# An attention-and-experts kernel on one core: the head shared out anew, expert registers loaded before the gathered rows, token tiles in order of time, and all closing sums on VectorE

## The chip, the cores and the metric

One core of a Trainium2 chip. The metric is device time in microseconds (us), the median of the runs. Engines are named as in the profile: PE is TensorE (PEld its weight loads), DVE is VectorE, ACT is ScalarE, POOL is GpSimd, SP is SyncE, which here only issues transfers.

## What is computed

Input x has 2 sequences of 2048 tokens with 128 channels, 4096 tokens in all.

```
xn  = layernorm(x)
xm  = xn * time_mix + shift(xn) * (1 - time_mix)
k, v, r = exp(min(xm Wk', 60)), xm Wv', xm Wr'
wkv, sum_k = decayed running sums over time of k*v and of k
s   = (sigmoid(r) * wkv / sum_k) Wo'
e   = argmax(xn Wg + bg)            (one of 8 experts for each token)
g   = silu(relu(xn W1[e] + b1[e]) W2[e] + b2[e])
out = x + s * g
```

All matrices are float32. W1[e] is 128x512 and W2[e] 512x128.

## The kernel before, in words

The 4096 tokens are 32 tiles of 128 (`NT`), four tiles to a block of 512 (`TPB`, 8 blocks `NB`, 4 to a sequence, `NBB`). A block's tokens are dealt to partitions four in a row: partition p of block c holds tokens 4p to 4p+3, so that a load or a store of a block is one run of 2 KB on each partition. The helper `every(a, j)` takes each fourth column of a block, and puts a tile's columns back in order of time where a tile meets a transposed block: in `transposes` (output in PSUM), in `logits_by_token` and in `project` (stationary operand in SBUF).

Head. SP loads x in 8 pieces, then the projection weights, biases, W1 and W2. DVE takes the statistics of each tile (L499), in two halves; after each half it works out `rstd` and `nbias` (L505 to L523) with one square root on ACT (`deviation`, L770). The tiles are then normalised by three engines: of each block POOL does tiles 0 and 1 (L452), ACT tile 2 (L786), DVE tile 3 (L533). POOL comes to it behind its series for the decay (L435 to L444). PE transposes the tiles (`transposes`, L939), ACT copies them out (L793), PE forms the gate logits (L948), ACT copies those (L805), PE turns them by token (L957), and DVE picks experts and makes ranks and one-hot tables (L573 to L640). PE inverts the order with 32 small matmuls (L1028), after the first `INV_AFTER` = 8 of 24 k/v/r projections (`kvr`, L989). From this come `gidx` (rows to gather), `etab` (the expert of each slot), `ttab` and `sidx`. The normalised rows go to DRAM as `xn_rows` (L351), behind the load of W2 on SP's queue.

Loop. There are 39 slots (`SLOTS`): rows sorted by expert, 128 to a slot, some tiles run twice. POOL gathers rows (L460), PE transposes them (L1038), multiplies by W1 of the slot's expert (`layer1`, L1047), ACT applies bias and relu (L857), PE multiplies by W2 (`layer2`, bias at L1059, L1064), ACT copies (L866), POOL scatters to `g_rows` (L467). The first 12 slots also carry one projection each. The slot's expert sits in a register; registers are loaded eight at a time (`Picks.fetch_for`, L95). The first load on PE stands behind `transpose_rows(0)`, and `layer2` and `relu` form the index `e*HC+c` for each of their four parts. Meanwhile DVE does the running sums (`attend`).

Tail. When all scatters have landed, SP loads `g_rows` in 8 blocks (L370), ACT applies silu (L917), DVE multiplies by the projected attention (L748) that PE makes with 64 matmul passes (`project`, L1079), and x is added: by DVE (L753) for blocks 0, 2, 4, 6, 7, by POOL (L483) for blocks 1, 3, 5 (`POOL_SUMS`). SP stores each block (L376).

Of the kernel before, what the change touches and what calls it, by code (L numbers as in the profile page):

```python
# [31 lines left out]
POOL_SUMS = (1, 3, 5)  # L32
# [13 lines left out]
XLOADS = NB  # L46
# [4 lines left out]
INV_AFTER = 2 * NBB  # L51
# [4 lines left out]
TAYLOR = 9  # L56
SMALL_DECAY = 0.5
# [3 lines left out]
BK = 3 * BQ  # L61

# [40 lines left out]
def mixture_kernel(nc, x, time_decay, time_first, time_mix, Wk, Wv, Wr, Wo, Wg, bg, W1, b1, W2, b2, out):  # L103
    ctx = ExitStack()
    with ctx:
# [24 lines left out]
        w2 = sb("w2", [P, E * HC, P])  # L130
        wnat = sb("wnat", [P, 4, P])
# [11 lines left out]
        b1T = sb("b1T", [P, BQ])  # L143
        tmix = sb("tmix", [P, 1])
# [164 lines left out]
        out_pool = sem("out_pool")  # L309
# [20 lines left out]
        def _(sp):  # L330
            for j in range(XLOADS):
                sp.dma_start(x_sb[:, j * TPB:(j + 1) * TPB, :], x_v[:, j, :, :]).then_inc(ld_x[j], 16)
# [12 lines left out]
            sp.dma_start(w2[:, :, :], W2.rearrange("e (c p) d -> p (e c) d", p=P)).then_inc(ld_w2, 16)  # L345

            for b in range(BATCH):
                sp.wait_ge(xn_pool, NBB * (b + 1))
                sp.wait_ge(xn_dve, NBB * (b + 1))
                sp.wait_ge(xn_act, NBB * (b + 1))  # L350
                sp.dma_start(xn_v[:, b * NBB:(b + 1) * NBB, :, :],  # L351
                             xn_sb[:, b * HALF:(b + 1) * HALF, :].rearrange("p (c j) d -> p c j d", j=TPB)
                             ).then_inc(xn_stored, 16)
# [14 lines left out]
            for c in range(NB):  # L368
                tiles = slice(c * TPB, (c + 1) * TPB)
                sp.dma_start(g_sb[:, tiles, :], g_v[:, c, :, :]).then_inc(g_loaded[c], 16)  # L370
            for c in range(NB):
                if c in POOL_SUMS:
                    sp.wait_ge(out_pool, POOL_SUMS.index(c) + 1)
                else:
                    sp.wait_ge(out_dve, len([m for m in range(c + 1) if m not in POOL_SUMS]))
                sp.dma_start(out_v[:, c, :, :],  # L376
# [381 lines left out]
        def _(act):  # L758
# [51 lines left out]
            for k in range(NBB):  # L810
                normalise(k)
# [326 lines left out]
```

## Time and profile before

| what | value |
|---|---|
| median of 3 runs | 176.46 us (175.15 to 176.85) |
| the profiled execution, time | 175.93 us |
| its span, first to last instruction | 174.1 us, mean granted PE clock 0.963 |
| busy: PE, DVE, ACT, POOL | 149.5, 122.8, 102.4, 98.5 us |
| DMA moved | 27.96 MB, mean 161 GB/s |

The 1.8 us between span and time lie outside the instructions. Busy shares are averages over three stages with different limits: the head to about 45 us, the loop to about 153 us, and the tail.

### The profile page before, as it was taken

The page shows a single profiled execution, that of the slowest core. Times are in us where ns is not written, and L with a number is a line of the kernel's source. Part 1 is how long each engine was busy: PE and PEld are TensorE (multiplying, and loading weights), DVE is VectorE, ACT ScalarE, POOL GpSimd, SP SyncE. Part 2 cuts the span into 40 slices and gives each one's busy share as a digit, 9 for nine tenths or more (in the row PEclk, how much of TensorE's full clock was granted, in tenths as well). Part 3 has the DMA queues.
Part 4 walks back from the last instruction along what each step waited for, and adds up shares of the span by engine and source line. Part 5 has one row for each costly group of instructions (what it writes and reads, how often), then busy time and mean ns, then how long its engine had stood idle before and what let it go on. Part 6 is the DMA issues. An engine that isn't in the chain of part 4 may idle for free.

```text
span 174.1 us, 3350 instructions
## 1 busy us (share of the span) xinstructions
PE 149.5 (86%) x954; PEld 119.0 (68%) x954; DVE 122.8 (71%) x262; ACT 102.4 (59%) x295; POOL 98.5 (57%) x149
## 2 busy tenths in 40 slices
PE   7995899996797689995999794985999999999960
PEld 2433465442575477874789693885999999999960
DVE  2498994999999999999999999999600000000971
ACT  2946975976484366564782922744886677642720
POOL 7879920017777475764455876746564464460550
PEclk9999999999699969999699999999999999999997
DMA  4943999706354142342323631543645552115973
GB/s 80 318 155 136 386 295 341 292 3 210 106 166 124 34 161 90 109 168 85 111 86 116 211 105 49 171 147 105 230 153 178 175 178 96 45 45 184 361 297 120
DMA packets 15808, 27.96 MB, mean 161 GB/s; under 512 B 2952, under 2 KB 3520, under 8 KB 15792
## 3 DMA queue, kind: packets, MB, share of 16 engines
q1 hardware_dynamic: 12944, 23.10, 37.7%
q0 software_dynamic: 2272, 4.66, 9.5%
q8 instruction: 8, 0.13, 0.3%
q10 hardware_dynamic: 576, 0.01, 0.2%
q14 instruction: 8, 0.07, 0.1%
HBM read 10.78 MB, written 6.75 MB: 101 GB/s over the span
## 4 chain that ended last, share of the span: by engine, by line
PE 66%; issue 7%; ACT 6%; DMA 5%; POOL 4%; DVE 4%; another core or an unknown queue 3%; ACTq 2%; DVEq 0%
PE ps L1064 21%; PE ps L1047 20%; PE ps L1079 9%; PE ps L989 7%; DMA wg<-in_L_ffn_Wg 3%; PE ps L948 3%; DMA xg<-xn_rows,gidx 2%; PE ps L1038 2%; PE ps L939 2%; PE ps L1059 1%; ACT ohhi_hidif L857 1%; POOL ser L441 1%; DVE ohlo L607 1%; ACT kT L875 1%
## 5 line engine op out<-in xcount | busy, mean ns | idle before, releaser
L467 POOL DMA_INDIRECT g_rows<-gout,sidx x39 | 40.1, 1028 | 25.4 <-ACT gout L866 18.6
L460 POOL DMA_INDIRECT xg<-xn_rows,gidx x32 | 34.0, 1064 | 33.3 <-DVE gidx L658 15.8
L1047 PE MATMUL ps<-xn_sb,w1e 128*128 x312 | 43.7, 282 | 3.8 <-issue 3.7
L1047 PEld LDWEIGHTS ps<-xn_sb,w1e 128*128 128x128 f32 x312 | 39.9, 198 | 4.6 <-issue 4.6
L857 ACT ACTIVATE ohhi_hidif<-ps,b1T 128x128 f32<-128x128 f32 x104 | 30.2, 384 | 19.1 <-PE ps L1047 16.9
L1064 PE MATMUL ps<-w,ohhi_hidif 128*128 x208 | 29.6, 282 | 2.5 <-issue 2.5
L748 DVE TENSOR_TENSOR kT<-ps,kT 128x512 f32<-128x512 f32 x8 | 5.3, 688 | 37.3 <-ACT kT L917 36.4
L989 PE MATMUL ps<-xmT,wT 128*128 128x512 f32 x48 | 25.7, 649 | 4.5 <-ACT rT L877 1.9
L1064 PEld LDWEIGHTS ps<-w,ohhi_hidif 128*128 128x128 f32 x208 | 25.6, 192 | 5.6 <-issue 5.3
L866 ACT COPY gout<-ps 128x128 f32<-128x128 f32 x39 | 11.1, 284 | 15.7 <-remote 10.1
L857 ACT ACTIVATE hidT<-ps,b1T 128x128 f32<-128x128 f32 x52 | 15.0, 380 | 8.3 <-remote 4.2
L1064 PE MATMUL ps<-w,hidT 128*128 x104 | 16.2, 305 | 0.1
L1064 PEld LDWEIGHTS ps<-w,hidT 128*128 128x128 f32 x104 | 14.4, 214 | 1.9 <-issue 1.8
L1079 PE MATMUL ps<-wT,xnT 128*128 128x128 f32 x64 | 15.1, 397 | 0.0
L1079 PEld LDWEIGHTS ps<-wT,xnT 128*128 128x128 f32 x64 | 15.0, 330 | 0.0
L989 PEld LDWEIGHTS ps<-xmT,wT 128*128 128x128 f32 x48 | 8.3, 198 | 9.5 <-issue 5.6
L717 DVE RECIPROCAL ohlo<-ohlo 128x256 f32<-128x256 f32 x8 | 14.0, 1747 | 0.0
L721 DVE RECIPROCAL ohlo<-ohlo 128x256 f32<-128x256 f32 x8 | 13.9, 1741 | 0.0
L927 PE MATMUL ps<-ones 128*128 128x512 bf16 x46 | 11.8, 421 | 1.0 <-POOL ones L386 1.0
L499 DVE BATCH_NORM_STATS2 stats<-x_sb 128x6 f32<-128x128 f32 x32 | 7.3, 280 | 5.3 <-DMA x_sb<-in_L_attn_x 5.3
L698 DVE TENSOR_TENSOR_SCAN zk<-ps,zk,kT 128x512 f32<-128x512 f32 x8 | 10.2, 1276 | 0.0
L927 PEld LDWEIGHTS ps<-ones 128*128 128x128 bf16 x46 | 4.8, 106 | 7.5 <-issue 2.2
(165 smaller groups left out, 220.1 us busy)
## 6 DMA issues: line engine op xcount, KB each, us to landing
w1e<-w SPq DMA_DIRECT2D x39, 256.0 KB
x_sb<-in_L_attn_x SPq DMA_DIRECT2D x8, 256.0 KB, 6.1
w<-in_L_ffn_W SPq DMA_DIRECT2D x1, 2048.0 KB, 9.5
xn_rows<-xn_sb SPq DMA_DIRECT2D x2, 1024.0 KB, 12.4
kT<-g_rows SPq DMA_DIRECT2D x8, 256.0 KB, 4.4
out_x<-kT SPq DMA_DIRECT2D x8, 256.0 KB, 2.1
g_rows<-gout,sidx POOLq DMA_INDIRECT x39
xg<-xn_rows,gidx POOLq DMA_INDIRECT x32
```

Source lines behind the costliest of these rows:

```text
L460: g.indirect_dma_start(xg[j][:, :], None, xn_rows, bass.IndirectOffsetOnAxis(gidx[:, s:s + 1], 0)).then_inc(gathered[j], 16)
L467: g.indirect_dma_start(g_rows, bass.IndirectOffsetOnAxis(sidx[:, s:s + 1], 0), gout[j][:, :], None).then_inc(scattered[j], 16)
L698: v.tensor_tensor_scan(zk[:, 1:BLK + 1], decay(BLK), kT[:, here], zk[:, 0:1], ALU.mult, ALU.add).then_inc(dve_step, 1)
L717: v.reciprocal(rden[:, 0:BLK // 2], den[:, 0:BLK // 2]).then_inc(dve_step, 1)
L721: v.reciprocal(rden[:, half_b], den[:, half_b]).then_inc(dve_step, 1)
L857: last = s.activation(hidT[n % DEEP][:, cols], psH[n % DEEP][:, cols], ACT.Relu, bias=b1T[:, bass.ds(experts.of(n) * HC + c, 1)])
L866: s.copy(gout[n % OUT_RING][:, :], Y_BANK[n][:, 0:P]).then_inc(g_ready, 1)
L927: t.matmul(psS[:, :], ones[:, :], ones[:, 0:1].to_broadcast([P, BLK]), start=True, stop=True)
L989: last = t.matmul(bank_of(m)[:, :], wT[:, w, :], xmT[:, c * BLK:(c + 1) * BLK], start=True, stop=True)
L1047: last = t.matmul(psH[n % DEEP][:, cols], w1e[n % W1_RING][:, cols], xgT[:, bass.ds(held.of(n), 1), :].rearrange("p o t -> p (o t)"), star ...
L1064: last = t.matmul(Y_BANK[n][:, 0:P], hidT[n % DEEP][:, cols], w2[:, bass.ds(e * HC + c, 1), :].rearrange("p o d -> p (o d)"), start=False, ...
L1079: last = t.matmul(S_BANK[q][:, j * P:(j + 1) * P], every(rw[q], j), wT[:, 3, :], start=True, stop=True)
```

## The change

- Tokens: tile n is now 128 consecutive tokens, one to a partition. `every` goes; the transposes and the projection read and write 128 neighbouring columns. Loads of x and g, and the stores of xn and of the output, touch DRAM in runs of 512 B, four for what was one of 2 KB.
- Head: POOL normalises before its decay series, and also takes over the splitting of the b2 bias (8 small operations) from DVE. Tiles to engines: `POOL_TILES`, `DVE_TILES`, `ACT_TILES`, in all 12, 10 and 10 instead of 16, 8 and 8. ACT does `deviation(1)` ahead of its first copy, and mixes later. PE transposes the projection weights first. The inversion stands behind 10 projections instead of 8. The store of `xn_rows` goes ahead of the load of W2.
- Registers: on PE the loads for the first slots stand ahead of `transpose_rows(0)`, and `layer2` and `relu` index by the expert alone with a fixed part for c. The wait for W2 moves to slot 2.
- Tail: all eight closing sums on DVE.

```
-POOL_SUMS = (1, 3, 5)
-INV_AFTER = 2 * NBB
+TANH_AFTER = 2 * NBB
+INV_AFTER = TANH_AFTER + 2
+POOL_TILES = [(0, 1)] * NBB + [(0,)] * NBB
+DVE_TILES = [(3,)] * 2 + [()] * 2 + [(1, 3)] * NBB
+ACT_TILES = [(2,)] * 2 + [(2, 3)] * 2 + [(2,)] * NBB
...
-        x_v = x.rearrange("b (c p j) d -> p (b c) j d", p=P, j=TPB)
-        out_v = out.rearrange("b (c p j) d -> p (b c) j d", p=P, j=TPB)
-        xn_v = xn_rows.rearrange("(c p j) d -> p c j d", p=P, j=TPB)
-        g_v = g_rows[0:TOK, :].rearrange("(c p j) d -> p c j d", p=P, j=TPB)
-        every = lambda a, j: a.rearrange("p (q j) -> p j q", j=TPB)[:, j, :]
+        x_v = x.rearrange("b (n p) d -> p (b n) d", p=P)
+        out_v = out.rearrange("b (n p) d -> p (b n) d", p=P)
+        xn_v = xn_rows.rearrange("(n p) d -> p n d", p=P)
+        g_v = g_rows[0:TOK, :].rearrange("(n p) d -> p n d", p=P)
...
             for c in range(NB):
-                if c in POOL_SUMS:
-                    sp.wait_ge(out_pool, POOL_SUMS.index(c) + 1)
-                else:
-                    sp.wait_ge(out_dve, len([m for m in range(c + 1) if m not in POOL_SUMS]))
+                sp.wait_ge(out_dve, c + 1)
...
             deviation(0)
             for k in range(NBB):
                 normalise(k)
-            copy_xnT(0)
             deviation(1)
+            copy_xnT(0)
+            act.wait_ge(wT_ps, 1)
+            s.copy(wT[:, :, :].rearrange("p t d -> p (t d)"), psW[:, :]).then_inc(wT_ready, 1)
             copy_xnT(1)
+            normalise(4)
+            normalise(5)
+            copy_xnT(2)
+            normalise(6)
+            normalise(7)
+            copy_xnT(3)
             act.wait_ge(ld_small, 16 * 2)
             mix_here(0)
...
                 for c in range(HC):
                     cols = slice(c * P, (c + 1) * P)
                     last = t.matmul(Y_BANK[n][:, 0:P], hidT[n % DEEP][:, cols],
-                                    w2[:, bass.ds(e * HC + c, 1), :].rearrange("p o d -> p (o d)"),
+                                    w2_e[:, bass.ds(e, 1), cols].rearrange("p o d -> p (o d)"),
                                     start=False, stop=c == HC - 1)
...
-                    last = t.matmul(S_BANK[q][:, j * P:(j + 1) * P], every(rw[q], j), wT[:, 3, :],
+                    last = t.matmul(S_BANK[q][:, j * P:(j + 1) * P], rw[q][:, j * P:(j + 1) * P], wT[:, 3, :],
                                     start=True, stop=True)
...
             for m in range(INV_AFTER, EARLY):
                 kvr(m)
-            transpose_rows(0)
             pe.wait_ge(experts_ready, 1)
-            pe.wait_ge(bias_ready, 1)
-            pe.wait_ge(sel_ready, 3)
-            pe.wait_ge(ld_w2, 16)
             experts.fetch_for(0)
             pe.wait_ge(held_ready, 1)
             held.fetch_for(0)
+            transpose_rows(0)
+            pe.wait_ge(bias_ready, 1)
+            pe.wait_ge(sel_ready, 3)
```

## Rows read from the trace of the kernel before

**Rows 1.** The chain that ended last: start us, us, what.

```profile
13.72 1.80 POOL xn_sb L452 x4
...
21.72 0.75 PE ps L957 x4
22.47 0.44 PE ps L939 x4
...
40.19 3.18 DMA xg<-xn_rows,gidx
43.37 1.29 issue
...
153.45 14.95 PE ps L1079 x64
```

**Rows 2.** Groups by line and shape: busy us, mean ns, idle before.

```profile
L1047 PEld LDWEIGHTS ps<-xn_sb,w1e 128*128 128x128 f32 x312 | 39.9, 198 | 4.6 <-issue 4.6
...
L1079 PEld LDWEIGHTS ps<-wT,xnT 128*128 128x128 f32 x64 | 15.0, 330 | 0.0
```

**Rows 3.** VectorE in order of time in the tail: start us, us, operation.

```profile
160.76 1.32 DVE L748 TENSOR_TENSOR kT<-ps,kT 128x512 f32<-128x512 f32 x2 [35.94 <-ACT kT L917]
...
168.42 0.69 DVE L748 TENSOR_TENSOR kT<-ps,kT 128x512 f32<-128x512 f32 x1 [0.97 <-PE ps L1079]
169.03 1.28 DVE L753 TENSOR_TENSOR kT<-kT,x_sb 128x512 f32<-128x512 f32 x2
```

**Rows 4.** ScalarE in order of time in the tail.

```profile
160.00 1.28 ACT L917 ACTIVATE kT<-kT 128x512 f32<-128x512 f32 x2 [4.73 <-DMA kT<-g_rows]
162.37 3.90 ACT L917 ACTIVATE kT<-kT 128x512 f32<-128x512 f32 x6 [1.09 <-DMA kT<-g_rows]
```

**Rows 5.** DMA issues: count, KB each, median us to landing.

```profile
out_x<-kT SPq DMA_DIRECT2D x8, 256.0 KB, 2.1
```

**Rows 6.** Stretches: PE, PEld, DVE, ACT, POOL busy, granted clock, DMA share, GB/s.

```profile
22.00:30.00 8.00, 7.66 (x36) 4.55 (x36) 5.47 (x16) 5.11 (x10) 0.86 (x2) 1.00 1.05 313
30.00:33.00 3.00, 3.00 (x16) 1.47 (x15) 2.69 (x6) 2.91 (x6) 0.00 (x0) 1.00 1.05 409
```

**Rows 7.** VectorE in order of time, head, first half of x.

```profile
7.07 0.87 DVE L499 BATCH_NORM_STATS2 stats<-x_sb 128x6 f32<-128x128 f32 x4 [0.33 <-DMA x_sb<-in_L_attn_x]
...
8.42 0.15 DVE L553 TENSOR_SCALAR omt<-tmix 128x1 f32<-128x1 f32 x1 [0.48 <-DMA wg<-in_L_ffn_Wg]
```

**Rows 8.** ScalarE in order of time, head.

```profile
12.31 1.65 ACT L786 ACTIVATE xn_sb<-x_sb,nbias,rstd 128x128 f32<-128x128 f32 x4 [1.72 <-DVE nbias L523]
15.36 0.59 ACT L793 COPY xnT<-ps 128x512 f32<-128x512 f32 x1 [1.40 <-PE ps L939]
15.84 0.31 ACT L770 ACTIVATE std<-var,eps 128x16 f32<-128x16 f32 x1
```

**Rows 9.** PE in order of time, around the inversion.

```profile
31.99 4.54 PE L989 MATMUL ps<-xmT,wT 128*128 128x512 f32 x10
36.45 0.97 PE L1028 MATMUL ps<-ohhi_hidif,ohlo 128*128 128x32 f16 x24
37.66 0.36 PE L1028 MATMUL ps<-ohhi_hidif,ohlo 128*128 128x32 f16 x8 [0.24 <-DVE ohlo L607]
```

**Rows 10.** Register loads (L95): ns min/median/max, first and last start us.

```profile
L95 PEldq TENSOR_LOAD <-etab x5: 596/849/1546, 41.8 to 130.3; - x5
...
L95 PEldq TENSOR_LOAD <-ttab x5: 587/590/1125, 43.4 to 131.2; - x5
```

**Rows 11.** Stretches of the loop; columns as in group 6.

```profile
45.00:121.00 76.00, 64.20 (x428) 53.47 (x429) 75.70 (x128) 40.83 (x137) 49.54 (x47) 0.93 0.36 119
121.00:153.00 32.00, 32.00 (x288) 31.79 (x288) 3.82 (x6) 23.70 (x91) 17.38 (x18) 1.00 0.41 143
```

**Rows 12.** One line's instructions (L1064), its register operations.

```profile
L1064 PEldq FUSED_REGOPS  x156: 55/55/60, 51.6 to 152.2; - x156
```

**Rows 13.** A stretch at the start of the loop; columns as in group 6.

```profile
45.00:50.00 5.00, 5.00 (x22) 3.62 (x23) 4.96 (x13) 2.92 (x9) 4.09 (x4) 0.66 0.34 105
```

More of the change, by code:

```diff
@@ L45 @@
 SPARE = NS * P
-XLOADS = NB
+XLOADS = 8
 STAT = 6
@@ L61, with tiles_upto @@
 BK = 3 * BQ
+def tiles_upto(tiles, k):
+    return sum(len(tiles[m]) for m in range(k + 1))
 class Steps:
@@ L432, in _ @@
             g.tensor_copy(wgpad[:, :, 0:E], wg[:, :].unsqueeze(1).to_broadcast([P, TPB, E])).then_inc(wg_ready, 1)
+            for k in range(NB):
+                if k % NBB == 0:
+                    pool.wait_ge(ln_ready, k // NBB + 1)
+                for j in POOL_TILES[k]:
+                    n = k * TPB + j
+                    g.tensor_scalar(xn_sb[:, n, :], x_sb[:, n, :], rstd[:, n:n + 1], nbias[:, n:n + 1],
+                                    ALU.mult, ALU.add).then_inc(xn_pool, 1)
             pool.wait_ge(dec_ready, 1)
@@ L526, in finish_stats @@
                 dve.wait_ge(ln_ready, h + 1)
-            own_tiles = [n for n in range(NT) if n % TPB == 3]
+            own_tiles = [k * TPB + j for k in range(NB) for j in DVE_TILES[k]]
+            in_first = tiles_upto(DVE_TILES, NBB - 1)
             def normalise_tile():
@@ L557, in _ @@
             finish_stats(0, go_on=stats_tile)
-            for _ in range(len(own_tiles) // 4):
+            for _ in range(in_first):
                 normalise_tile()
@@ L749, in _ @@
                                     ALU.mult).then_inc(prod_ready, 1)
-                if c and c - 1 not in POOL_SUMS:
+                if c:
                     cols = slice((c - 1) * TPB, c * TPB)
@@ L811, in _ @@
                 normalise(k)
+            deviation(1)
             copy_xnT(0)
[L813 removed]
+            act.wait_ge(wT_ps, 1)
+            s.copy(wT[:, :, :].rearrange("p t d -> p (t d)"), psW[:, :]).then_inc(wT_ready, 1)
             copy_xnT(1)
+            normalise(4)
[4 more added lines that the diff above has]
+            copy_xnT(3)
             act.wait_ge(ld_small, 16 * 2)
             mix_here(0)
[L817 to L821 removed]
             act.wait_ge(ld_bg, 16 * TPB)
@@ L877, in copy_kvr @@
                     s.activation(rT[:, here], ps[:, :], ACT.Tanh, scale=0.5).then_inc(kvr_out, 1)
-            for m in range(INV_AFTER):
+            for m in range(TANH_AFTER):
                 copy_kvr(m)
@@ L883, in _ @@
             s.activation(sqrt_eps[:, :], eps[:, :], ACT.Exp)
-            for m in range(INV_AFTER, EARLY):
+            for m in range(TANH_AFTER, EARLY):
                 if m == EARLY - 1:
@@ L938, in transposes @@
                 for j in range(TPB):
-                    last = t.transpose(every(psT[k % 2][:, :], j), xn_sb[:, k * TPB + j, :], ident[:, :])
+                    last = t.transpose(psT[k % 2][:, j * P:(j + 1) * P], xn_sb[:, k * TPB + j, :], ident[:, :])
                 last.then_inc(xnT_ps, 1)
@@ L956, in logits_by_token @@
                 for i in range(TPB):
-                    last = t.transpose(psB[h][:, i * P:(i + 1) * P], every(lgT[:, h, :], i), ident[:, :])
+                    last = t.transpose(psB[h][:, i * P:(i + 1) * P], lgT[:, h, i * P:(i + 1) * P], ident[:, :])
                 last.then_inc(gates, 1)
@@ L990, in kvr @@
                 last.then_inc(kvr_ps, 1)
+            pe.wait_ge(ld_proj, 16 * 4)
+            for m in range(4):
+                last = t.transpose(psW[:, m * P:(m + 1) * P], wnat[:, m, :], ident[:, :])
+            last.then_inc(wT_ps, 1)
             transposes(0)
@@ L1008, in _ @@
             logits(7)
-            pe.wait_ge(ld_proj, 16 * 4)
-            for m in range(4):
-                last = t.transpose(psW[:, m * P:(m + 1) * P], wnat[:, m, :], ident[:, :])
-            last.then_inc(wT_ps, 1)
             logits_by_token(1)
```

95 lines of the change are left out of this document (37 added, 58 removed).

## The prediction

> **What bounds the kernel now.** I read the chain that ended last first, then each stage by the view that shows its limit. The chain is one path through three stages. In the head it runs over POOL's normalising, which starts at 13.72 although ACT had its numbers at 12.31, on through PE's transposes and logits, over DVE's tables and the inversion on PE, to the gathered rows: the second gather takes 3.18 us to 43.37, and the first matmul of the loop waits another 1.29 us for nothing that a semaphore shows [rows 1, 8]. The reader should see that the 1.29 us is PE's sequencer at two register loads, 1546 and 1125 ns at their slowest, the first of them at 41.8 [rows 10]. The loop has two parts: to 121 us PE works 64.20 of 76 us, from 121 to 153 all of 32 us [rows 11]. The tail begins at 153.45 with 14.95 us of `project` [rows 1]. The averages mislead here: PE looks like the bound of the tail, but two other things run through it. The loads of g let the first silu start at 160.00 [rows 4], and the DVE operations behind it follow each other at 0.60 to 0.63 us (1.32 less 0.69 for a pair of products, 1.28 less 0.68 for a pair of sums), from 160.76 until 170.31 [rows 3]. PE holds DVE up only before the last product, by 0.97 us.
>
> **The tail, part by part.** (1) `project`'s weight load took 330 ns on average with every fourth column, against 198 with neighbouring columns in L1047 [rows 2]; the passes came at 14.95/64 = 0.234 us, against 32/288 = 0.111 us in the packed part of the loop, where the weights lie in neighbouring columns [rows 11]; I take 0.12. So `project` shrinks to 64 x 0.12 = 7.6 us and ends near 161.1 instead of 168.4. By itself that is no gain of 7 us: what is late next is DVE. (2) DVE now has 16 operations instead of 13. I lay them out: product 0 at 160.76, product 1 at 161.39, sum 0 at 161.99; product 2 can't start before its silu ends, 162.37 plus (3.90/6) = 163.02 [rows 4], so it starts at 163.10; behind it stand 6 sums (1 to 6) and 5 products (3 to 7), then sum 7: 13 operations with product 2. Twelve steps of 0.60 put the last sum at 170.3 and its end at 171.0. Before, DVE ended at 170.31. So the tail loses 0.7 us by its own sum, although PE is freed by 7: three sums at 0.6 = 1.8 us eat the 0.97 us of waiting and more. Cover that is gone: POOL's adds were wholly hidden. (3) The loads and stores now touch DRAM in 512 B runs. W2's load already has such runs: around it (22 to 30 us, queues full) the DMAs moved 313 GB/s, right behind it with the 2 KB runs of `xn_rows` 409 GB/s [rows 6], a factor 1.31. On the last store, which lands in 2.1 us [rows 5], that is +0.3 us (bounds 0 and 1.31 x 2.1 = +0.65). The 4.2 MB of loads and stores need 4.2/0.313 = 13.4 us from about 158.5, that is to 171.9, ahead of the last store's landing near 173.5; so the queue isn't the bound, but close to it. Tail: +1.0 us, bounds +0.3 (sums packed a little denser, no cost of the runs) and +1.9 (silus late by the slower loads as well).
>
> The Trainium skill (DMA: Bandwidth & Descriptors, the table at its head) gives 512 B and above as enough for line rate, by which the runs of 512 B cost nothing. The two stretches above speak against it for this kernel. By it the tail would lose 0.7 us and the head's 0.6 us below would be nil.
>
> **The head.** (4) x arrives in 512 B runs. Third and fourth pieces matter: DVE waited for the third until 7.07, and then for the small constants until 8.42 [rows 7]. Between 5 us and there the transfers are what is waited for; 1.31 times as long puts the third piece at about 7.7 and the fourth at about 9.1, where its statistics now start at 8.5, right behind L553. +0.6 us (bounds 0, where the constants still come last, and +1.2). (5) POOL can now start at 12.3 instead of 13.72, so transposes stand ready 1.4 us earlier. But ACT now does `deviation(1)` ahead of the first copy, and that waits for the second half's statistics: it ran at 15.84, behind two fillers of DVE that are gone, so about 15.5; the first copy, at 15.36 before, comes at about 15.9 [rows 8]. With it, ACT's copy of wT and the four normalisings (0.39 us each, 1.65 for four) between the copies, the first logits come out 0 to 0.3 us later than before, not 1.4 earlier. The transposes that POOL frees have their cover in ACT's order. (6) The two `logits_by_token` took 0.75 us for four, with neighbouring columns they take 0.44 as L939 does [rows 1]: -0.6 us. Parts 5 and 6: -0.4 us, bounds -1.0 and +0.6.
>
> L939 also wrote PSUM with a stride, and still took 0.44 us for four [rows 1]. The Trainium skill (SBUF — State Buffer, the paragraph on cachelines) says that any access to PSUM that isn't contiguous slows matmuls markedly. By that rule the eight `transposes` would gain as `logits_by_token` does, some 0.3 us each where on the path; by the row I give them nothing.
>
> (7) The inversion now stands behind 10 projections. Before, it started at 36.45 exactly where the eighth ended and where its first table was ready, and its last part waited 0.24 us for DVE [rows 9]. Ten passes took 4.54 us with the last one drawn out, some 0.43 us from start to start, two to a projection, so two projections are 1.7 us: projections end 1.7 us later, the 32 small matmuls then run through in 1.3 us, and the result comes at about 39.5 instead of 38.0. +1.4 us (bounds +0.9, if PE starts this stretch earlier relative to DVE since wT is ready, and +1.7). Queued behind it are `gidx` on DVE, all of POOL's gathers, and SP's and ACT's register loads. (8) The register loads ahead of the rows: PE now loads while the gathers fly, the 1.29 us goes [rows 1]. What is late next is the second gather itself, so -1.3 us is the most, -0.6 the least. (9) Splitting b2 on POOL, the decay series later, `xn_rows` ahead of W2: all nil; POOL then idled from about 23 us to the gather at 38.6, W2 is first wanted in the loop, and DVE didn't lag there. If that cover went, the split would cost some 3 us before the gather. Head: 0.6 - 0.4 + 1.4 - 1.3 = +0.3 us.
>
> **The loop.** L1064 ran 156 register operations, 4 a slot, of 55 ns [rows 12]; `relu` forms its index 4 times a slot on ACT too. From 121 to 153 us PE is packed with them all in place [rows 11], so there they cost nothing. In the 11.8 us that PE stood idle before 121 some waits have no releaser in the trace; whether fewer register operations help there no row says. I take 0, bounds -4 (a third of the idle time) and +1.5 (such waits falling worse).
>
> **The sum** against the profiled execution: 175.93 + 1.0 (tail) + 0.3 (head) + 0 (loop) = 177.3 us. That execution is 0.5 us under the median of the runs and inside their spread, so 177.3 stands for the median too, 0.5% above it. No change can be told from one within 1% (174.7 to 178.2).
>
> **The rivals.**
> - *The loop's idle time shrinks.* Fewer instructions in PE's and ACT's streams, and a loop that begins without the 2.8 us gap that preceded a granted clock of 0.66 [rows 13]. For: waits without releaser fall inside L1064 and L1047. Against: the packed part. 3.5 us of the 11.8: 177.3 - 3.5 = 173.8.
> - *The runs of 512 B cost nothing* (the skill's rule): 177.3 - 0.6 - 0.3 = 176.4. Against it, rows 6; those stretches differ in more than the run, so it keeps a chance.
> - *It doesn't do what it says*: `project` stays bound by its weight loads. Then DVE waits for PE as now and only the last sums and the runs remain: tail +0.3, 176.6.
> - *Slower: PE's clock falls in the head.* Transposes 0 and 1 are now done by about 15.3 and PE waits for ACT's first copy until 16.5 or, with x late, 17.1; with the gap after the warm-up matmuls it works little from 12.8 to 17. PE's gap from 41.8 to 44.66 [rows 1, 10] preceded the stretch at 0.66 of full clock [rows 13], that is partly at 1.2 GHz. If it falls here, the four logits and two transposes on the path, 4 x 2 passes of 0.43 [rows 9] + 2 x 0.44 [rows 1] = 4.3 us, run at half speed for most of their length: +2 us, 179.3. It decides from the point where the first copy is later than about 17.
>
> **How the numbers follow.** Forecast 0.42 (its own range 175.6 to 178.9), shrinking loop 0.22, free runs 0.11, no faster weights 0.05, clock 0.20. The range 173.4 to 180.0 takes in all centres and the bounds of the tail and head, and leaves out the far end of the loop's. Faster by over 1%: the 0.22 and a little of the forecast, 0.25. Slower by over 1%: 0.20 and the upper quarter of the forecast, 0.32. Within 1%: 0.43.
>
> **What will show it.** L1079's passes at 0.12 us and PE done near 161 while the last DVE operation ends later than 170.31; 16 DVE operations from about 160.8 almost without a gap; the fourth piece of x waited for at about 9; GB/s near 310 where x, xn and g move; the first ACT copy at about 16.5 behind L770; the inversion's end 1.4 us behind the last table; no gap for register loads ahead of the loop. The forecast is wrong if the loop from its first L1047 to the first L1079 isn't 108.5 us within 1.5, if the granted clock leaves 1.0 in the head, or if the g loads rather than DVE order the tail.

## The result and the profile after

The changed kernel takes 182.03 us (median; 180.44 to 185.0) against 175.86 for the kernel before (175.15 to 176.85), a ratio of 1.039 with an interval of 1.031 to 1.048. The forecast was 177.3 with a range up to 180.0, so the loss is real and larger than anything the range allowed. The profiled execution took 182.01 us with a span of 179.9; 174.1 was the span before.

Split the span at two instructions, the first pass of the expert loop and the first pass of `project`, and the place of the loss is plain:

| | before | after | difference | forecast |
|---|---|---|---|---|
| head, to the first pass of L1047 / L1044 | 44.9 | 44.9 | 0.0 | +0.3 |
| loop, to the first pass of L1079 / L1076 | 108.4 | 113.6 | +5.2 | 0 |
| tail, to the end of the span | 20.8 | 21.4 | +0.6 | +1.0 |

The loop of the kernel before is counted here to 153.29, where the first pass starts by the records; the chain's 153.45 gives the 108.5 of the prediction.

The tail came out within 0.4 us of what was written. Groups by line and shape, after (columns as in [rows 2]):

```profile
L1076 PEld LDWEIGHTS ps<-wT,xnT 128*128 128x128 f32 x64 | 7.2, 192 | 0.0
```

The weight load fell from 330 to 192 ns, and the 64 passes end 7.3 us behind their start at 158.49. VectorE in order of time in the tail, after (answers to [rows 3]):

```profile
166.29 1.49 DVE L742 TENSOR_TENSOR kT<-ps,kT 128x512 f32<-128x512 f32 x2 [40.22 <-ACT kT L914]
167.70 0.68 DVE L747 TENSOR_TENSOR kT<-kT,x_sb 128x512 f32<-128x512 f32 x1
168.97 0.69 DVE L742 TENSOR_TENSOR kT<-ps,kT 128x512 f32<-128x512 f32 x1 [0.59 <-ACT kT L914]
...
175.57 1.28 DVE L747 TENSOR_TENSOR kT<-kT,x_sb 128x512 f32<-128x512 f32 x2
```

It never waits for PE; after its one wait of 0.59 us for ScalarE it is packed and ends at 176.85, 18.4 us behind the start of `project` against 17.0 before. ScalarE shows why it starts late (answers to [rows 4]):

```profile
165.53 0.63 ACT L914 ACTIVATE kT<-kT 128x512 f32<-128x512 f32 x1 [5.06 <-DMA kT<-g_rows]
166.35 0.63 ACT L914 ACTIVATE kT<-kT 128x512 f32<-128x512 f32 x1 [0.19 <-DMA kT<-g_rows]
168.24 0.63 ACT L914 ACTIVATE kT<-kT 128x512 f32<-128x512 f32 x1 [1.25 <-DMA kT<-g_rows]
```

Seven silus wait for a piece of g, two did before [rows 4]. The DMA issues of the page say the same, against 4.4 us for g before and 2.1 for the stores [rows 5]:

```profile
kT<-g_rows SPq DMA_DIRECT2D x8, 256.0 KB, 5.2
out_x<-kT SPq DMA_DIRECT2D x8, 256.0 KB, 2.6
```

The head, by the chain that ended last, after (start us, us, what):

```profile
37.91 0.81 PE ps L1025 x32
...
38.74 0.20 DVE gidx L652
38.94 0.03 POOLq L486
38.97 0.83 issue
39.80 1.37 POOL xg L475
...
41.47 3.04 DMA xg<-xn_rows,gidx
44.51 0.14 issue
```

The wait of 1.29 us for register loads [rows 1] is 0.14 here; the first gather starts at 39.80, where before it started at 38.6. Steps (7) and (8) can both be read off. Now the loop, by stretches (columns as in [rows 6]; answers to [rows 11] and [rows 13]), after:

```profile
45.00:50.00 5.00, 5.00 (x21) 3.86 (x21) 4.96 (x11) 3.16 (x10) 3.78 (x5) 0.55 0.37 120
52.00:66.00 14.00, 7.83 (x37) 5.83 (x37) 13.93 (x23) 4.88 (x15) 6.42 (x8) 0.78 0.27 89
45.00:121.00 76.00, 62.75 (x422) 53.23 (x422) 74.99 (x127) 40.54 (x135) 47.34 (x47) 0.90 0.35 114
```

and the same middle stretch of the kernel before:

```profile
52.00:66.00 14.00, 10.61 (x60) 8.45 (x59) 13.93 (x24) 6.03 (x20) 9.69 (x10) 0.88 0.33 105
```

Between 52 and 66 us PE makes 37 matmuls instead of 60. What happens there, ScalarE in order of time (its L854 is `relu`), after:

```profile
52.37 0.40 ACT L846 COPY xn_sb<-ps 128x256 f32<-128x256 f32 x1
59.03 1.14 ACT L854 ACTIVATE hidT<-ps,b1T 128x128 f32<-128x128 f32 x4 [6.26 <-remote]
```

and before:

```profile
53.69 1.14 ACT L857 ACTIVATE hidT<-ps,b1T 128x128 f32<-128x128 f32 x4 [1.43 <-remote]
55.20 0.59 ACT L875 COPY kT<-ps 128x512 f32<-128x512 f32 x1 [0.37 <-remote]
59.56 0.27 ACT L866 COPY gout<-ps 128x128 f32<-128x128 f32 x1 [3.77 <-remote]
```

and PE, after:

```profile
51.14 1.06 PE L1044 MATMUL ps<-xn_sb,w1e 128*128 x8
...
54.00 1.06 PE L1044 MATMUL ps<-xn_sb,w1e 128*128 x8
61.22 2.08 PE L986 MATMUL ps<-xmT,wT 128*128 128x512 f32 x2 [6.17 <-ACT kT L872]
```

and SyncE, which waits for the same semaphore before it issues the next copy of W1, after:

```profile
59.02 0.49 SPq L370 DMA_DIRECT2D w1e<-w  x1
```

"Remote" is the profile's word where it finds no releaser. The `relu` at 59.03 is that of the third slot (the `relu`s of the first two start at 47.08 and 50.36). It waits for `hid_ps`, and by the records the third slot's W1 passes ended at 52.20. Two engines that wait for this semaphore go on within 0.01 us of each other, 6.8 us later. So ScalarE isn't what is slow: the signal itself, PE's, comes late, or the passes ended later than the records say, for the ends of matmuls are modelled. PE's next projection then waits for ScalarE until 61.22. Before has such waits of ScalarE in three parts, 5.6 us together. PE stands idle for 6.2 of these 14 us after and for 3.4 before, and that difference alone is larger than the whole forecast.

A count of matmuls in a window depends on where it ends (from 45 to 121 us it is 422 against 428 [rows 11], for the kernel before stands still twice just ahead of 121), so here is the lag of the changed kernel slot by slot, at the first W1 pass: 0.0 us at the first slot, 3.7 at the seventh, 3.1 at the 24th, 5.2 at the 26th, and 5.2 at the last. So 3.7 of the 5.2 us are lost before the seventh slot, and the rest around the 25th, where PE stops three times between 121.8 and 124.4 us, for 2.05 us in all.

The register operations that I hoped would be fewer are not. One line's instructions, after:

```profile
L1061 PEldq FUSED_REGOPS  x156: 46/46/46, 52.2 to 157.3; - x156
```

Still 156, 46 ns each where they took 55 [rows 12].

### The profile page after: what moved, and what is told of

Read it like the earlier page. It is cut to its first block, busy times and chain, and to the rows that moved or that the text cites. A ratio compares the mean times of both kernels' runs of the same rounds, so it can differ in the third digit from the quotient of the medians.

```text
span 179.9 us, 3350 instructions
## 1 busy us (share of the span) xinstructions
PE 143.1 (80%) x954; PEld 113.6 (63%) x954; DVE 122.9 (68%) x259; ACT 102.9 (57%) x297; POOL 93.8 (52%) x150
## 3 DMA queue, kind: packets, MB, share of 16 engines
q1 hardware_dynamic: 25232, 23.10, 39.8%
## 4 chain that ended last, share of the span: by engine, by line
PE 59%; DMA 8%; ACT 8%; DVE 7%; issue 6%; another core or an unknown queue 5%; POOL 2%; ACTq 2%; SPq 1%; DVEq 0%; POOLq 0%
PE ps L1044 20%; PE ps L1061 19%; PE ps L986 10%; PE ps L945 4%; DMA wg<-in_L_ffn_Wg 3%; DMA kT<-g_rows 3%; ACT ohhi_hidif L854 2%; DVE stats L510 2%; PE ps L1035 2%; DVE kT L742 2%; DMA xg<-xn_rows,gidx 2%; DVE kT L747 1%; ACT hidT L854 1%; DMA g_rows<-gout,sidx 1%
## 5 line engine op out<-in xcount | busy, mean ns | idle before, releaser
L482 POOL DMA_INDIRECT g_rows<-gout,sidx x39 | 39.8, 1021 | 27.7 <-ACT gout L863 22.5
L475 POOL DMA_INDIRECT xg<-xn_rows,gidx x32 | 33.1, 1036 | 31.3 <-DVE gidx L652 10.9
L1044 PE MATMUL ps<-xn_sb,w1e 128*128 x312 | 45.0, 288 | 2.5 <-issue 2.5
L1044 PEld LDWEIGHTS ps<-xn_sb,w1e 128*128 128x128 f32 x312 | 41.3, 205 | 3.3 <-issue 3.1
L854 ACT ACTIVATE ohhi_hidif<-ps,b1T 128x128 f32<-128x128 f32 x104 | 29.9, 377 | 20.5 <-PE ps L1044 18.5
L742 DVE TENSOR_TENSOR kT<-ps,kT 128x512 f32<-128x512 f32 x8 | 5.5, 688 | 40.9 <-ACT kT L914 40.8
L1061 PE MATMUL ps<-w,ohhi_hidif 128*128 x208 | 30.7, 293 | 1.4 <-issue 1.4
L1061 PEld LDWEIGHTS ps<-w,ohhi_hidif 128*128 128x128 f32 x208 | 27.2, 203 | 4.6 <-issue 4.3
L854 ACT ACTIVATE hidT<-ps,b1T 128x128 f32<-128x128 f32 x52 | 15.1, 380 | 13.4 <-remote 6.3
L1061 PE MATMUL ps<-w,hidT 128*128 x104 | 15.4, 294 | 0.0
L1061 PEld LDWEIGHTS ps<-w,hidT 128*128 128x128 f32 x104 | 13.5, 203 | 1.3 <-issue 1.2
L1056 PE MATMUL ps<-b_rows,sel 96*128 96x128 bf16 x39 | 8.9, 229 | 3.1 <-ACT gout L863 3.1
L1035 PE MATMUL ps<-ident,xg 128*128 128x128 f32 x32 | 7.4, 312 | 3.7 <-DMA xg<-xn_rows,gidx 3.7
```

Of the source, the lines that this page charges most:

```text
L475: g.indirect_dma_start(xg[j][:, :], None, xn_rows, bass.IndirectOffsetOnAxis(gidx[:, s:s + 1], 0)).then_inc(gathered[j], 16)
L482: g.indirect_dma_start(g_rows, bass.IndirectOffsetOnAxis(sidx[:, s:s + 1], 0), gout[j][:, :], None).then_inc(scattered[j], 16)
L854: last = s.activation(hidT[n % DEEP][:, cols], psH[n % DEEP][:, cols], ACT.Relu, bias=b1T_e[:, bass.ds(experts.of(n), 1), c:c + 1].rearran ...
L1035: last = t.transpose(psX[:, (n - first) * P:(n - first + 1) * P], xg[n % RING][:, :], ident[:, :])
L1044: last = t.matmul(psH[n % DEEP][:, cols], w1e[n % W1_RING][:, cols], xgT[:, bass.ds(held.of(n), 1), :].rearrange("p o t -> p (o t)"), star ...
L1061: last = t.matmul(Y_BANK[n][:, 0:P], hidT[n % DEEP][:, cols], w2_e[:, bass.ds(e, 1), cols].rearrange("p o d -> p (o d)"), start=False, sto ...
```

## The experiments

Two things must be known to read them. The kernels of one set ran on one chip, and the chips are not alike: on two of the chips of these sets, as in the runs of the result, the kernel before takes 176 to 177 us; on the three others 157. So each ratio is against the kernel before on the same chip, and sets are not mixed. And a single profile stands for each run, while ratios rest on several executions.

### First set: the parts one by one (kernel before: 157.38 us)

e1, the kernel before with the new token layout and nothing else:

```
-x_v = x.rearrange("b (c p j) d -> p (b c) j d", p=P, j=TPB)
+x_v = x.rearrange("b (n p) d -> p (b n) d", p=P)
-last = t.matmul(S_BANK[q][:, j * P:(j + 1) * P], every(rw[q], j), wT[:, 3, :],
+last = t.matmul(S_BANK[q][:, j * P:(j + 1) * P], rw[q][:, j * P:(j + 1) * P], wT[:, 3, :],
```

> The kernel before with the new token layout alone (loads, stores, transposes, projection and the order of the tokens; head, registers and sums as before). Theory A (the 512 B runs of the layout pay for most of the loss, in the g loads, and the projection's gain finds no use): +1.5 to +3 us on 175.9, g loads landing at about 5.2 us each where it was 4.4, loop from the first L1047 to the first projection pass near 108.5 us. Theory B (the loss of 5 us sits in the loop and comes from how the loop is entered: register loads ahead of the rows, projections before the inversion): -1 to +1 us, loop 108.5 us. Theory C (the order of the tokens itself makes gathers and the loop slower): +5 us, loop near 113 us.

e2, the changed kernel with the old layout (the same lines the other way).

> The changed kernel with the old token layout (four tokens to a partition, 2 KB runs, strided projection), all else as changed. Theory A: about 178 to 179, the g loads at 4.4 us, but the tail again bound by 15 us of projection. Theory B: 181 to 182, loop near 113.5 us. Theory C: 177, loop near 108.5 us.

e3, the changed kernel with three of the closing sums on GpSimd again:

```
+POOL_SUMS = (1, 3, 5)
```

> The changed kernel with the closing sums of blocks 1, 3 and 5 back on POOL. If VectorE's order bounds the tail (my sum: three sums at 0.6 us): -1.5 us against the changed kernel. If the landings of the g loads bound it, which came 0.85 us apart in the changed kernel: -0.6 us or less. The loop is not touched under any theory.

e4, the changed kernel with the register loads behind the first transposes and the old index form again:

```
+transpose_rows(0)
+pe.wait_ge(bias_ready, 1)
+pe.wait_ge(sel_ready, 3)
+pe.wait_ge(ld_w2, 16)
 ...
-transpose_rows(0)
-b1T_e[:, bass.ds(experts.of(n), 1), c:c + 1]
+b1T[:, bass.ds(experts.of(n) * HC + c, 1)]
```

> The changed kernel with registers as before: loads behind the first transposed rows, index e*HC+c, wait for W2 before the loop. Theory A and C: +1 us (the loop begins 1.3 us later), loop length unchanged near 113.5 us. Theory B: the loop falls back to about 108.5 us, total 178 to 179.

| | time | ratio to before | interval | span | last VectorE operation to the end |
|---|---|---|---|---|---|
| e1 layout alone | 157.87 | 1.004 | 1.001 to 1.007 | 155.1 | 4.8 |
| e2 all but the layout | 157.86 | 1.001 | 0.997 to 1.005 | 155.6 | 2.5 |
| e3 all but VectorE's sums | 159.24 | 1.011 | 1.005 to 1.017 | 157.2 | 4.8 |
| e4 all but the registers | 159.18 | 1.011 | 1.005 to 1.017 | 157.1 | 3.1 |

The expectations named times near 176 us, so on this chip only their differences can be read, and the changed kernel itself isn't in this set. No part costs 4% here, and none of these traces has a hole like the one above. The gain of step (8) is seen in e4 against e2: with the register loads behind the rows the loop starts at 46.25 against 45.29 us, and `project` at 136.25 against 135.25.

The weight load fell to 192 ns with the layout alone (330 in e2), and it bought nothing. What it met in the tail are two other things, and four traces part them. From VectorE's last operation to the end it takes 4.8 us in e1 and e3 (512 B runs, GpSimd's sums kept), 3.1 in e4 (512 B runs, all sums on VectorE), 2.5 in e2 (2 KB runs, all sums on VectorE) and 3.8 in the trace of the kernel before, on a slower chip (2 KB runs, GpSimd's sums). So the shorter runs cost 0.6 to 1.0 us there and GpSimd's sums 1.3 to 1.7. In e1 GpSimd's last sum, of block 5, starts at 147.31 and takes 1.64 us, and the stores go out in the order of the blocks, so those of blocks 5, 6 and 7 leave together. Against that VectorE's end comes about 1 us later with all the sums (16.5 and 16.9 us behind the start of `project` in e1 and e3, 17.8 in e2 and e4). In sum, moving the sums to VectorE didn't lengthen the tail with 512 B runs, where the prediction has it do so: 21.4 and 21.8 us in e1 and e3 with GpSimd's sums, 20.9 in e4 without; on slower chips 22.4 in e7 and 22.4 in e6. The runs of 512 B by themselves, e4 against e2 on one chip: a piece of g lands after 4.8 us against 4.4, a store after 2.7 against 2.1, and the tail is 0.5 us longer.

### Second set: the changed kernel again, the inversion, the sums (kernel before: 177.21 us)

> The changed kernel itself, to be compared on the chip of this call with the kernel before. The first four experiments ran both parents at 157 to 159 us, where the pair of the result was at 176 and 182, and their traces have hardly any waits without a releaser in the loop. Theory L (most of the 5 us lost in the loop are such waits, which are a matter of the chip and fall otherwise in each kernel): here +1.0 to +1.5%, 158.9 to 159.8 us. Theory B (the way into the loop costs 5 us on any chip): +3% or more.

> The kernel before itself, for its trace on this chip: loop from the first L1047 to the first projection pass near 90 us under theory L, its head as in the trace shown (first L1047 at about 44.9 us), tail bound by the projection. Ratio 1.00.

e5, the changed kernel with the inversion where it was:

```
-INV_AFTER = TANH_AFTER + 2
+INV_AFTER = TANH_AFTER
```

> The changed kernel with the inversion behind 8 projections again. By my step 7 (the inversion waits for two projections) the first L1047 comes 0.7 to 1.4 us earlier than in the changed kernel and the time falls by as much. If the register loads or the gathers' own pace hold the loop's start: no change.

e6, the kernel before with the layout and all sums on VectorE (`POOL_SUMS` gone):

> The kernel before with the new token layout and all sums on VectorE. Against the layout alone (+0.4%): +0.5 to +1 us if VectorE's order bounds the tail, nil if the landings of the g loads do.

The changed kernel gave 181.62 us, 1.028 (1.018 to 1.037); the kernel before against itself 1.009 (1.002 to 1.015), which is how far such a comparison can be off on this chip (its profiled execution took 178.25 us, where the median of its ten is 176.9); e5 179.9, 1.018 (1.007 to 1.028); e6 177.14, 0.999 (0.994 to 1.005). So layout and sums together are free, and what is left for the loss is the head's order, the inversion and the registers. The kernel before itself has a loop of 111.3 us in this profile, where the first had 108.4. Ten projections ahead of the inversion cost what was forecast: in e5 the loop starts at 43.86, 45.20 in the changed kernel, 1.3 us. But putting it back didn't take the hole away.

### Third set: are the stalls VectorE's doing? (kernel before: 176.32 us)

In the traces so far of the slower chips PE's last gaps ended at 119 to 125.5 us, little before VectorE's running sums (`attend`) did, at 124 to 127, and PE was packed from there on. I took that for a cause.

x1, the changed kernel with these sums behind the loop:

```
+cap_keys(1)
+dve.wait_ge(hid_ps, SLOTS - 1)
```

> The changed kernel, but VectorE waits for the second-last slot of the expert loop before its running sums, so they no longer run beside the loop; output unchanged, the sums then stand between loop and projection. Theory A (TensorE and ScalarE stall in the loop only where VectorE works at its running sums beside them): the loop from the first L1047 to its last slot's matmuls falls from 112 to 114 us to 88 to 92, with hardly a gap over 0.55 us, and the time rises all the same, by about 40 to 60 us, since the sums come behind. Theory B (the stalls belong to the loop's own work: instruction fetch, transfers of gather and scatter, the clock): the loop keeps its 20 us of gaps. If before runs near 157 us in this call, no stalls are there to take away and the loop is about 90 us by both.

x2, the changed kernel, and x3, the kernel before, with the sums' numerators and decay in SBUF:

```
-decay_ps, num = psG[:, 0:1], psG[:, 1:BLK]
+decay_ps, num = sb("decay_sb", [P, 1])[:, :], ohlo_f[:, 2 * BLK:3 * BLK - 1]
```

> The changed kernel with the decay and numerators of VectorE's running sums in SBUF in place of the PSUM bank psG. Theory A1 (VectorE's reads and writes of PSUM hold up the matmuls): the loop loses most of its 20 us of gaps, 160 to 168 us where the changed kernel has 180 to 182. Theory A2 (the stalls go with VectorE's sums wherever they lie, in SBUF too, or with its instruction stream): 178 to 184, gaps near 21 us. Where before runs near 157: between 157 and 160 by both.

> The kernel before with the same move of decay and numerators from PSUM to SBUF. Theory A1: loop 90 to 95 us in place of 108, time 158 to 164. Theory A2: 175 to 179, ratio to before 0.99 to 1.01. Where before runs near 157: ratio 0.99 to 1.01 by both.

e7, the kernel before with the layout and the registers ahead:

> The kernel before with the new token layout and the register loads ahead of the rows; order of the head, place of the inversion, sharing of the normalising and POOL's sums as before. Theory C (the cost of the change comes with the later inversion and the reordered head, which shift VectorE's sums against TensorE's slots): first L1047 about 1.0 us earlier than before's, near 43.5, loop 106 to 109 us, time ratio 0.98 to 1.0. Theory D (the token layout with the registers' new place, another index form and code, disturbs the loop by itself): loop 111 to 114 us and ratio 1.01 to 1.03. Where before runs near 157: 0.99 to 1.0 by C.

x1 took 251.06 us (ratio 1.43). Its stretches, the third and fourth column pair being VectorE and ScalarE:

```profile
52.00:66.00 14.00, 7.04 (x35) 4.63 (x34) 0.00 (x0) 5.53 (x18) 6.68 (x7) 0.83 0.30 95
66.00:125.00 59.00, 52.36 (x373) 46.42 (x373) 1.23 (x1) 33.37 (x112) 35.29 (x36) 0.92 0.36 121
```

VectorE does next to nothing, and PE makes 35 matmuls from 52 to 66 as with it (37), 373 from 66 to 125 as with it. ScalarE's hole is there too:

```profile
61.83 1.14 ACT L854 ACTIVATE hidT<-ps,b1T 128x128 f32<-128x128 f32 x4 [4.71 <-remote]
```

The theory is dead: PE's gaps end at 125.2 us without VectorE's sums too. x2 (179.18, 1.020; 1.008 to 1.032) and x3 (177.42, 1.004; 0.993 to 1.015) fit that. e7 gave 177.63, 1.014 (1.002 to 1.026): its loop starts at 43.0, 1.2 us earlier than e1's and 1.0 earlier than e6's, which is step (8) as forecast, and its time gains nothing from it. Its loop of 110.2 us lies between what its two theories had (106 to 109 and 111 to 114), so it decides between them for neither.

All profiles of the slower chips side by side, matmuls in two stretches, and the time from the first slot's first W1 pass to the seventh's and from there to the last slot's. Two traces of the other chips stand below for comparison:

| | span | first gather | 52 to 66 us | 66 to 125 us | first to seventh slot | seventh to last |
|---|---|---|---|---|---|---|
| kernel before | 174.1 | 38.6 | 60 | 374 | 23.1 | 81.4 |
| kernel before again | 176.4 | 38.3 | 45 | 371 | 25.1 | 82.3 |
| x3 | 175.0 | 38.3 | 68 | 366 | 22.6 | 83.1 |
| e6 | 173.6 | 38.0 | 55 | 385 | 22.5 | 80.8 |
| e7 | 175.6 | 38.0 | 48 | 373 | 24.4 | 81.8 |
| changed kernel | 179.9 | 39.8 | 37 | 366 | 26.8 | 82.9 |
| changed kernel again | 179.5 | 40.0 | 28 | 373 | 28.5 | 79.8 |
| e5 | 176.7 | 38.7 | 28 | 380 | 27.9 | 79.8 |
| x2 | 178.7 | 40.9 | 50 | 363 | 25.9 | 80.7 |
| x1 (sums behind the loop) | 249.4 | 40.9 | 35 | 373 | 27.7 | 81.5 |
| e1, no stalls | 155.1 | 38.0 | 99 | 508 | 17.3 | 68.3 |
| changed kernel (z2 below), no stalls | 156.3 | 40.1 | 99 | 498 | 17.2 | 68.9 |

The two columns at the right tell it. To the seventh slot the five kernels with the old head need 22.5 to 25.1 us, the five with the new one 25.9 to 28.5, 3.8 us more on average and without overlap. From there to the last slot both kinds need the same, 81.9 and 80.9 us. (e7 has the registers ahead and stands with the old head, e5 has the inversion back and stands with the new one.) So most of the loss is a hole at the loop's start, not a slower loop. The 12 us by which the rest of the loop is slower here than on the other chips fall on both kernels alike. In the ten traces ScalarE's third `relu` starts at 53.0 to 55.8 us with the old head and at 55.0 to 61.8 with the new one; where it comes after 59, SyncE goes on within 0.05 us of it. In z2 it comes 0.5 us behind the records of its passes, at 52.35.

### Fourth and fifth set: are they GpSimd's gathers? (kernel before: 157.3 and 157.28 us)

In nine of the ten traces ScalarE's long waits at the loop's start end 0.2 to 2.4 us behind the first 14 gathers, which GpSimd issues one behind the other. In eight of the ten, PE's last gap over 0.55 us in the loop ended 2.7 to 4.5 us behind the start of the last gather (in x2 and in the kernel before again it came before it). So I changed the gathers.

y1, the changed kernel with plain copies, which bring each slot other rows than its own, so that the output is no longer that of the reference:

```
-g.indirect_dma_start(xg[j][:, :], None, xn_rows,
-                     bass.IndirectOffsetOnAxis(gidx[:, s:s + 1], 0))
+g.dma_start(xg[j][:, :], xn_rows[s * P:(s + 1) * P, :])
```

> The changed kernel, but GpSimd's 32 gathers by index are plain copies of rows 128s to 128s + 127 of xn_rows from the same queue, with the same waits and sizes, so each slot computes on other rows than it should. Theory G (TensorE and ScalarE are held up while GpSimd issues its gathers by index back to back, 14 of them from 40 to 58 us): ScalarE's hole of 6 to 8 us that ends at 59 to 62 us goes, slot 5 starts 9 to 10 us behind slot 3 in place of 15 to 17, and the loop shortens by 5 us or more. Theory H (the hole belongs to the loop's own first slots and projections): slot 5 starts 14 to 17 us behind slot 3 as before. Where before runs near 157 us there is no hole to take away.

y2 and y6, the changed kernel with `SCATTER_LAG = 3` and `9` in place of 5:

> The changed kernel with SCATTER_LAG 3 in place of 5: the first burst of gathers has 12 in place of 14 and the first scatter comes two gathers sooner. Theory G: the burst and the hole end some 2.5 us sooner, slot 5 starts 12 to 13 us behind slot 3, time 2 us less than the changed kernel's ratio of 1.03 to 1.04. Theory H: no difference, ratio to before 1.03 to 1.04.

> The changed kernel with SCATTER_LAG 9 in place of 5: up to 18 gathers before the first scatter. Theory G: the hole lasts longer, by what GpSimd's longer run of gathers allows (each pair behind the tenth waits for TensorE), slot 5 starts 16 to 20 us behind slot 3, time 1 to 4 us above the changed kernel's. Theory H: slot 5 as in the changed kernel, 14 to 17 us behind slot 3, time within 1% of it.

y3, the changed kernel with 4 buffers for gathered rows in place of 8:

> The changed kernel with 4 buffers for gathered rows in place of 8: the first burst has 4 gathers, then each pair waits for TensorE's transposes, 10 gathers before the first scatter. Theory G: the hole ends about 5 us sooner or breaks up, and the later stalls, which end 3.4 us behind the last gather in every run so far, end with the last gather again, which is now issued for slot 28 in place of 24, so that the last gap over 0.55 us comes later in the loop, at slots 27 to 29. Theory H: hole as in the changed kernel, last gap at slots 22 to 24 as before.

They fell on a chip without stalls, and so did the repeat of y1 with the changed kernel beside it:

> The changed kernel with GpSimd's gathers by index replaced by plain copies of rows from the same queue (each slot computes on other rows than it should), once more, since the first time it ran on a chip where before takes 157 us and no stall is there to take away. If before runs near 177 us here: theory G (the gathers hold up TensorE and ScalarE) gives slot 5 at 9 to 10 us behind slot 3 and a loop of 90 to 105 us; theory H (the hole belongs to the loop's own first slots) gives 14 to 17 us and a loop of 108 to 114. If before runs near 157 again, 156 to 160 by both, and what makes the stalls stays open.

> The changed kernel itself, beside the run with plain copies. Where before runs near 177 us: ratio 1.03 to 1.04, loop 111 to 114 us, slot 5 some 15 to 17 us behind slot 3. Where before runs near 157 us: the loop's share of the loss is gone and head and tail alone are left, ratio 1.005 to 1.015, loop 89 to 91 us.

| | time | ratio | interval |
|---|---|---|---|
| y1 plain copies | 158.08 | 1.005 (of the medians) | |
| y2 lag 3 | 161.61 | 1.028 | 1.020 to 1.036 |
| y3 four buffers | 167.34 | 1.056 | 1.045 to 1.066 |
| y6 lag 9 | 160.65 | 1.020 | 1.011 to 1.029 |
| z1 plain copies | 156.84 | 0.994 | 0.991 to 0.998 |
| z2 changed kernel | 159.26 | 1.016 | 1.012 to 1.020 |

The question about the stalls stays open with that. But z2 shows something else: without any stall the change still costs 1.6%, 2.0 us between the medians, a little more than the 1.005 to 1.015 expected of it. GpSimd's waits from 60 to 130 us (what waited for what: us in total, times, longest), z2:

```profile
POOL g_rows L482 <- issue: 9.1, 30, 0.3
POOL xg L475 <- issue: 4.9, 16, 0.3
POOL g_rows L482 <- ACT gout L863: 0.9, 3, 0.3
POOL xg L475 <- PE ps L1035: 0.6, 2, 0.3
```

51 pauses and none over 0.3 us: GpSimd waits for nobody, it issues its 71 gathers and scatters one behind the other, one in 1.38 us on average, from 40.1 to the last scatter at 136.9, and the loads of g wait for that scatter. In e1 it runs from 38.0 to 135.2. PE is as full as GpSimd, in the same trace (columns as in [rows 6]):

```profile
66.00:125.00 59.00, 58.99 (x498) 55.45 (x497) 58.81 (x95) 43.05 (x156) 46.51 (x42) 1.00 0.50 169
```

So neither has slack on such a chip. The first gather's start, by the chain of e1:

```profile
37.53 0.11 DVE gidx L656
37.64 0.32 issue
37.97 1.26 POOL xg L458
```

and by that of z2:

```profile
39.01 0.20 DVE gidx L652
39.24 0.83 issue
40.08 1.36 POOL xg L475
```

2.1 us later: 1.5 for gidx (the inversion for the most part), 0.5 for a longer pause of GpSimd ahead of its first gather, 0.83 instead of 0.32, in all traces with the new head whose chain shows it; its cause I didn't test. Of these 2.1 us 1.0 is left where the loop starts (the register loads give back 1.2), 1.5 where `project` starts, 1.7 at the first load of g, and 1.2 at the end of the span. It isn't the whole 1.6% either: e2 has its first gather as late (40.17) and is level with the kernel before.

z1 tells less than it seems. With plain copies GpSimd needs 0.55 us for an issue instead of 0.97 (medians) and waits for the others:

```profile
POOL g_rows L481 <- ACT gout L862: 18.1, 20, 1.2
POOL xg L475 <- PE ps L1034: 7.1, 7, 1.7
```

The changed kernel falls from 159.26 to 156.84, under the kernel before. But the first rows land sooner too: in the profiles the loop starts 1.3 us earlier (43.93 against 45.23), and is only 0.8 us shorter (89.2 against 90.0). By these two traces GpSimd's pace costs the loop about 0.8 us. y2 and y3 show from the other side how little slack there is. PE's waits in y3, 46 to 125 us:

```profile
PE ps L1036 <- DMA xg<-xn_rows,gidx: 4.1, 4, 1.7
```

With fewer gathers issued ahead PE runs into GpSimd's pace, and the loop takes 98.4 us instead of 90.0. With lag 9 (y6) the loop keeps 89.6 us, but the scatters come late, the last one at 138.3. Neither lag is faster than 5.

On the slower chips GpSimd has slack, for PE and ScalarE fall behind it. Its waits, same stretch, changed kernel:

```profile
POOL xg L475 <- PE ps L1035: 9.0, 5, 3.3
POOL g_rows L482 <- ACT gout L863: 7.5, 7, 2.8
POOL xg L475 <- remote: 4.7, 4, 1.4
```

No version ran faster than the kernel before beyond the interval while still computing the whole reference: e2 (1.001) and e6 (0.999) are level with it.

## Why the prediction was wrong

The step that failed is "The loop": "I take 0, bounds -4 ... and +1.5". It was +5.2 in the profiled executions. The 11.8 us in which PE stood idle before 121 us [rows 11] were named, seen to have no releaser, and bounded above by a guess no row carried. The runs show how wide that term is: the kernel before itself has loops of 108.4 and 111.3 us in two profiles, +2.9 with nothing changed, and from the first slot to the seventh the new head needs 3.8 us more than the old one on average. With +3 as its upper bound the range would have reached 181.5, still under 182.03. What I can show: 3.7 of the 5.2 us are lost before the seventh slot, where the third slot's signal comes late from PE; it isn't made by VectorE's sums, layout and sums alone don't bring it (e6), the registers ahead don't (e7, by its 24.4 us), it is there with the inversion back (e5), and it is absent on three of the chips. It isn't W2 either, whose load now goes later and which PE waits for at the third slot: it has landed at 36.7 us. What I can't: which part of the new head lengthens it, and what the hole is. One more rival was named in the expectation of x1 and never tested, the loading of instructions: in ten traces with the hole and three without I find one 16 KB packet of the instruction queue between 50 and 58 us, so the packet alone doesn't make a hole.

Two signs of being wrong that the prediction gives itself came true, the loop off by more than 1.5 us, and loads of g that order the first three products. The range was missed by the loop alone.

Without the stalls the forecast for head and tail, +1.3 us, stands against 2.0 measured (z2). The head is where it is short, +0.3 forecast and +1.0 in z2 against e1 and by the means below: (7) and (8) came as written, but (9) put nothing for GpSimd's pause of 0.5 us, and of the 0.6 us of (6) a quarter came.

The steps one by one:

- (1) `project` in 7.6 us: 7.3. Right.
- (2) VectorE's end +0.7 counted from the start of `project`: 18.4 us against 17.0, +1.4. The spacing of 0.60 was right; the first and third product came late through the loads of g. That three sums more on VectorE lengthen the tail was wrong for the new layout: 20.9 us in e4, 21.4 and 21.8 in e1 and e3. GpSimd's adds weren't "wholly hidden", they held the last stores back.
- (3) runs of 512 B: 1.31 times as long, +0.3 on the last store. Pieces of g 5.2 against 4.4 us, stores 2.6 against 2.1: 1.18 and 1.24. The tail's sum, +0.6 against +1.0, was right with its terms shifted. The Trainium skill (DMA: Bandwidth & Descriptors, the table at its head) has 512 B as enough for line rate; on one chip, e4 against e2, stores landed after 2.7 and 2.1 us and pieces of g after 4.8 and 4.4, so here the measurement speaks against it.
- (4) x in 512 B runs, +0.6: it came out the other way. The statistics of the fourth piece start at 7.91, where before they started at 8.49 behind the small constants [rows 7].
- (5) `deviation(1)` at 15.5, the first copy at 15.9: 15.17 and 15.38. The order of the argument was right.
- (6) `logits_by_token` 0.66 us for four instead of the 0.44 I took, 0.75 before: a quarter of the gain. The 0.44 was a misreading: the chain shows only the part of L939 that lies on it. From first start to last end its four take 0.60 us, in both kernels, so a gain of 0.15 was there to be had.
- (7) +1.4: 1.3 by e5. Right. (8) -1.3: -1.2 by e7 against e1, -1.0 by e2 against e4. Right as a start of the loop.
- (9) nil: not quite, GpSimd's 0.5 us ahead of its first gather.
- Head: +0.3; 0.0 in the profiled pair, but 44.1 to 44.9 for the loop's start in five traces with the old head and registers and 44.9 to 45.9 in ten of the changed kernel's kind (e4, e5 and the two with plain copies aside), +1.0 by the means.

Of the rivals, the shrinking loop had its sign wrong: register operations did not become fewer. The clock rival placed its trouble in the right region for the wrong reason. The granted clock was 0.55 from 45 to 50 us (0.66 before, [rows 13]), and 0.68 from 45 to 52; but z2 has 0.76 from 45 to 52 and e4 has 0.50 from 45 to 50, both without a hole, and e5 has 1.00 from 45 to 50 and the hole all the same. So a low clock there doesn't make it.

## What to carry to other kernels

When an idle time has no releaser in the trace, it is the least certain term of any forecast: take a second profile of the same kernel, see how much it moves by itself, and give it that much on both sides. When a wait has no releaser, look for another engine that waits for the same semaphore; if both go on at the same moment, it is the sender that is late. Compare two loops slot by slot, not by matmuls in a window. When one event feeds two engines, write down both paths to the end with the count of instructions on each; here 71 issues of 1.38 us on GpSimd, "not the bottleneck" by its busy share of 52%, were as long as PE's work wherever PE didn't stall. And a faster weight load is worth looking up behind it first: `project` lost half its time, and the loads, the sums and the stores behind it took all of it.

## What the runs showed of the hardware

- The same kernel takes 157.3 us on three chips and 176 to 177 on two others and in the runs of the result. From 52 to 66 us PE made 96 to 100 matmuls in every trace of the first kind and 28 to 68 in those of the second.
- The stalls of the second kind hit PE and ScalarE at once, at a semaphore whose matmuls are done by the records, and keep ScalarE waiting for up to 8.3 us (e5). SyncE, at the same semaphore, goes on at the same time (59.02 and 59.03 us in the changed kernel). They don't depend on VectorE (x1), nor on whether its sums lie in PSUM or SBUF (x2, x3). Whether the gathers make them wasn't settled: both runs with plain copies met chips without them.
- A gather or scatter by index costs GpSimd 0.97 us (median) and a pause of 0.3; a plain copy from the same queue 0.55 (y1, z1).
- A weight load with every fourth column took 330 ns against 192 with neighbouring ones (e2, e1). Transposes that wrote PSUM with that stride took 272 ns, as did those with neighbouring columns (L939 before, L936 after).
